# Attention projection's weights split in six parts inside head pairs 2 to 4, and its first row block's product laid in four pieces into the attention's drain

## What is computed

```python
h = _ln(x, ln1_g, ln1_b)
q, k, v = (einsum('btd,hds->bhts', h, W) for W in (Wq, Wk, Wv))
att = softmax(where(causal, q @ k.T * d ** -0.5, -inf))
out = (att @ v).transpose(0, 2, 1, 3).reshape(b, t, d)
x = x + out @ Wp + bp                  # the attention projection
h2 = _ln(x, ln2_g, ln2_b)
w, sel = top_k(h2 @ Wg, 1)             # the gate: one expert for each token
y = relu(h2 @ W1[sel] + b1[sel]) @ W2[sel] + b2[sel]
```

## Time and profile before

| | |
|---|---|
| median of 3 runs | 899.28 us (898.9 to 900.07) |
| the profiled execution | 897.33 us |
| its span | 895.8 us |
| PE busy | 850.7 us, 95% |
| DVE busy | 711.0 us, 79% |
| ACT busy | 553.0 us, 62% |
| attention's last head pair, from its first scores | 345.78 us on |
| first matmul of the projection | 383.26 us |
| first matmul of the experts | 444.39 us |

### The profile page before, as it was taken

One profiled execution on the slowest core, in us unless ns is written; L12 is line 12 of the kernel. 1 busy time (PEld: TensorE's weight loads), 2 busy tenths in 40 slices (PEclk: granted clock), 3 DMA queues, 4 the chain that ended last, 5 costly groups with the idle time before them and its releaser, 6 DMA issues.

```text
span 895.8 us, 14645 instructions
## 1 busy us (share of the span) xinstructions
PE 850.7 (95%) x5342; PEld 820.7 (92%) x5342; DVE 711.0 (79%) x1093; ACT 553.0 (62%) x783; POOL 80.1 (9%) x85
## 2 busy tenths in 40 slices
PE   6999999999999998799999999999999999999997
PEld 6989999999888887699899999999999999999996
DVE  6999676863687767734779798898989989898995
ACT  3612341353667667611678787787878888787870
POOL 2000000330400000022330000000000000000040
PEclk9999999999999999899999999999999999999998
DMA  7130008164810102730499999999999999999984
GB/s 197 40 106 1 19 10 168 53 175 89 334 54 2 54 1 70 227 89 2 130 357 350 372 334 372 355 359 378 342 379 367 358 373 354 376 354 371 367 279 135
DMA packets 116232, 196.00 MB, mean 219 GB/s; under 512 B 34052, under 2 KB 83420, under 8 KB 116182
## 3 DMA queue, kind: packets, MB, share of 16 engines
q1 hardware_dynamic: 107988, 169.08, 55.9%
q0 software_dynamic: 6368, 24.19, 8.0%
q10 hardware_dynamic: 1826, 2.06, 0.8%
HBM read 177.40 MB, written 17.90 MB: 218 GB/s over the span
## 4 chain that ended last, share of the span: by engine, by line
PE 52%; DVE 22%; DMA 14%; issue 6%; ACT 6%; SPq 0%; DVEq 0%; ACTq 0%
PE ps L1480 14%; DVE wlo L988 13%; DMA raw<-in_L_ffn_W 12%; PE ps L1874 7%; PE ps L1657 7%; PE ps L1855 6%; PE ps L1733 3%; ACT whi L658 2%; PE ps L1561 2%; PE ps L1587 2%; PE ps L1696 2%; PE ps L1711 2%; PE ps L1509 2%; DMA xs<-in_x 1%; DVE hTT L986 1%
## 5 line engine op out<-in xcount | busy, mean ns | idle before, releaser
L988 DVE TENSOR_TENSOR wlo<-raw,whi 128x2304 fp32r<-128x2304 f32 (+2 forms) x148 | 352.6, 2390 | 24.5 <-ACT whi L658 24.1
L658 ACT ACTIVATE whi<-raw 128x2304 fp32r<-128x2304 f32 (+2 forms) x150 | 300.4, 2004 | 80.0 <-DMA raw<-in_L_ffn_W 34.6
L1874 PE MATMUL ps<-whi,hTT 128*128 128x384 f32 x768 | 201.6, 339 | 1.0 <-ACT oh7T L658 1.0
L1874 PEld LDWEIGHTS ps<-whi,hTT 128*128 128x128 f32 x768 | 139.2, 188 | 1.2 <-ACT oh7T L658 1.2
L1855 PE MATMUL ps<-whi,hgh 128*128 128x384 f32 x384 | 133.1, 347 | 1.3 <-DVE hgl L988 1.3
L1855 PE MATMUL ps<-whi,hgl 128*128 128x384 f32 x384 | 129.1, 336 | 0.0
L1874 PE MATMUL ps<-wlo,hTT 128*128 128x384 f32 x384 | 129.0, 336 | 0.0
L1855 PE MATMUL ps<-wlo,hgh 128*128 128x384 f32 x384 | 128.4, 334 | 0.0
L1855 PEld LDWEIGHTS ps<-whi,hgh 128*128 128x128 f32 x384 | 72.2, 188 | 1.5 <-DVE hgl L988 1.5
L1874 PEld LDWEIGHTS ps<-wlo,hTT 128*128 128x128 f32 x384 | 72.3, 188 | 0.0
L1855 PEld LDWEIGHTS ps<-wlo,hgh 128*128 128x128 f32 x384 | 72.3, 188 | 0.0
(11 more groups left out here) (287 smaller groups left out, 1642.8 us busy)
## 6 DMA issues: line engine op xcount, KB each, us to landing
raw<-in_L_ffn_W SPq DMA_DIRECT2D x128, 1152.0 KB, 7.0
hs_d<-bc POOLq DMA_DIRECT2D x13, 384.0 KB, 6.4
raw<-in_L_gnn_W SPq DMA_DIRECT2D x4, 1152.0 KB, 6.3
hs<-hs_d POOLq DMA_DIRECT2D x8, 384.0 KB, 5.6
ys_d<-ysb POOLq DMA_DIRECT2D x7, 384.0 KB, 6.0
raw<-in_L_ffn_Wv SPq DMA_DIRECT2D x6, 384.0 KB, 5.5
raw<-in_L_ffn_Wq SPq DMA_DIRECT2D x12, 192.0 KB, 3.4
raw<-in_L_ffn_Wk SPq DMA_DIRECT2D x12, 192.0 KB, 3.3
```

What stands on the lines that cost most here:

```text
L658: act.activation(out_, in_, func).then_inc(s, 1)
L988: dve.tensor_tensor(out_, in_, hi_, ALU.subtract).then_inc(s, 1)
L1874: ins = mm(ps[0:CAP, 4 + half, 0:HB], l, rr, start=k == 0 and j == 0 and jj == 0, stop=k == FCH - 1 and j == JW - 1 and jj == 2)
```

## The change

The Wp split becomes six parts of 768 columns, in steps 14, 16, 17, 20, 22 and 24 (WP_AT). Each takes the place in `whi`/`wlo` and the third of `raw` that one unit had (WP_PLACE), and waits until that unit's products are done (WP_USED). Three of the last units change their place (UNIT_PLACE), and unit 11 is split in step 18 where it was in step 14. SP's second Wp load goes out after unit 11 and so four steps later; the experts' first chunk goes out after the third Wp part, in step 17, the second after the sixth, in step 24.

The product of row block 0 leaves the loop after the drain. Its 36 matmuls are four pieces of 9 (`first_block`): at the head of step 29, at the head of step 30, behind step 30's turns, and at the head of step 31. The six keep-busy matmuls go. The banks of the five blocks become 0, 2, 4, 6, 4 (WP_BANK), and the waits follow the banks: the first piece waits for all maxima (its banks held scores), for all six Wp parts and for the heads of row block 0; block 4 waits for block 2's residual, gate products for block 1's.

```diff
-UNIT_PLACES = 6
-UNIT_SLOT = (0, 0, 1, 1, 0, 1)
-UNIT_COL = (0, D, 0, D, 2 * D, 2 * D)
+UNIT_PLACE = (0, 1, 2, 3, 4, 5, 0, 1, 2, 3, 5, 2)
+RAW_PLACES = 6
+PLACE_SLOT = (0, 0, 1, 1, 0, 1)
+PLACE_COL = (0, D, 0, D, 2 * D, 2 * D)
-UNIT_AT = {1: 6, 4: 7, 6: 8, 9: 9, 11: 10, 14: 11}
+UNIT_AT = {1: 6, 4: 7, 6: 8, 9: 9, 11: 10, 18: 11}
-WP_PARTS = 4
+WP_AT = {14: 0, 16: 1, 17: 2, 20: 3, 22: 4, 24: 5}
+WP_PLACE = (0, 1, 4, 3, 5, 2)
+WP_USED = (16, 16, 16, 20, 22, 24)
+WP_BANK = (0, 2, 4, 6, 4)
+WP_QUARTER = 9
-WP_AT = STEPS - 6
-DRAIN_BUSY = 3
...
             def wp_hi(k):
-                n, part = divmod(k, WP_PARTS // 2)
-                if not k:
-                    a.wait_ge(s_pj, C + 4 * PAIRS)
+                p = WP_PLACE[k]
+                n = PLACE_SLOT[p]
+                a.wait_ge(s_pj, C + WP_USED[k])
                 a.wait_ge(s_raw[n], raw_value(2 * WP + n))
-                cols = slice(part * CH // 2, (part + 1) * CH // 2)
-                hi(front_w[n][0][:, cols], raw[n][:, cols], s_fhi)
+                hi(place(p, front_w)[0], raw[n][:, PLACE_COL[p]:PLACE_COL[p] + D], s_fhi)
...
+            def first_block(k):
+                if not k:
+                    pe.wait_ge(s_mx, 2 * STEPS)
+                    pe.wait_ge(*split(FRONT + 4))
+                    pe.wait_ge(s_pvl, 2 * (STEPS - C + 1))
+                order = {0: 0, 1: 1, 3: 2, 2: 3}[k]
+                for a_ in range(order * WP_QUARTER, (order + 1) * WP_QUARTER):
+                    half, a_m = divmod(a_, QK)
+                    m, i = divmod(a_m, 3)
+                    l, rr = pairs([t[:, m, 0:P] for t in q],
+                                  [t[:, half * HB:(half + 1) * HB] for t in wpart(2 * WP, m)])[i]
+                    ins = mm(ps[0:P, WP_BANK[0] + half, 0:HB], l, rr, start=a_m == 0, stop=a_m == QK - 1)
+                if order == 3:
+                    ins.then_inc(s_wp, 1)
...
-                if i >= STEPS:
-                    keep_busy(DRAIN_BUSY, v[0][:, 0, 0:128], v[0][:, 0, 0:512], 0)
+                if i >= STEPS - 1:
+                    first_block(i - STEPS + 1)
                 if 1 <= i <= STEPS:
                     turn(2 * i - 2)
                     turn(2 * i - 1)
+                if i == STEPS:
+                    first_block(3)
...
             for c in range(C):
+                if c == 4:
+                    pe.wait_ge(s_x2, 3)
+                if c:
+                    rows_product(q, 2 * WP, c, WP_BANK[c], {DC - 1: (s_pvl, 2 * STEPS)} if c == 1 else None
+                                 ).then_inc(s_wp, 1)
                 if c >= 2:
-                    pe.wait_ge(s_x2, c - 1)
-                rows_product(q, 2 * WP, c, 4 + 2 * (c % 2), None if c else {DC - 1: (s_pvl, 2 * STEPS)}).then_inc(s_wp, 1)
-                if c >= 2:
+                    if c == 2:
+                        pe.wait_ge(s_x2, 2)
                     gate_products(c - 2)
```

More of the change, by code:

```diff
@@ L311, in unit, with place @@
         def unit(j, tensors):
-            p = j % UNIT_PLACES
-            return [t[:, UNIT_COL[p]:UNIT_COL[p] + D] for t in tensors[UNIT_SLOT[p]]]
+            return place(UNIT_PLACE[j], tensors)
+        def place(p, tensors):
+            return [t[:, PLACE_COL[p]:PLACE_COL[p] + D] for t in tensors[PLACE_SLOT[p]]]
         def raw_unit(j):
-            return raw[j % UNIT_PLACES // 3][:, j % 3 * D:(j % 3 + 1) * D]
+            return raw[j % RAW_PLACES // 3][:, j % 3 * D:(j % 3 + 1) * D]
         def unit_count(j):
@@ L347, in build @@
         s_fhi, s_flo = sem("front_hi"), sem("front_lo")
-        s_unit = [sem(f"qk_weight_in{p}") for p in range(UNIT_PLACES)]
+        s_unit = [sem(f"qk_weight_in{p}") for p in range(RAW_PLACES)]
         s_uhi, s_ulo = sem("qk_weight_hi"), sem("qk_weight_lo")
@@ L481, in _ @@
                 m, r = divmod(j, 2)
[L482 to L483 removed]
+                if j >= RAW_PLACES:
+                    sp.wait_ge(s_ulo, unit_count(j - RAW_PLACES))
                 else:
@@ L498, in weights @@
                     elif n < F_RAWS:
-                        sp.wait_ge(*split(2 * WP + WP_PARTS // 2 * (n + 1)))
+                        sp.wait_ge(*split(2 * WP + 3 * (n + 1)))
                     else:
@@ L780, in unit_hi @@
             def unit_hi(j):
-                a.wait_ge(s_unit[j % UNIT_PLACES], 32 * (j // UNIT_PLACES + 1))
-                if j >= UNIT_PLACES:
-                    a.wait_ge(s_pj, C + 2 * (j - UNIT_PLACES) + 2)
+                a.wait_ge(s_unit[j % RAW_PLACES], 32 * (j // RAW_PLACES + 1))
+                held = [n for n in range(j) if UNIT_PLACE[n] == UNIT_PLACE[j]]
+                if held:
+                    a.wait_ge(s_pj, C + 2 * held[-1] + 2)
                 else:
-                    a.wait_ge(*USED[(GNN2, WV)[UNIT_SLOT[j]]])
+                    a.wait_ge(*USED[(GNN2, WV)[PLACE_SLOT[j]]])
                 hi(unit(j, front_w)[0], raw_unit(j), s_uhi)
@@ L874, in _ @@
                     unit_hi(UNIT_AT[i])
-                if 0 <= i - WP_AT < WP_PARTS:
-                    wp_hi(i - WP_AT)
+                if i in WP_AT:
+                    wp_hi(WP_AT[i])
                 if i % C in QK_LATE and window_pair(i) < PAIRS:
@@ L1218, in wp_lo @@
             def wp_lo(k):
-                n, part = divmod(k, WP_PARTS // 2)
+                p = WP_PLACE[k]
+                n = PLACE_SLOT[p]
                 d.wait_ge(s_fhi, 2 * WP + k + 1)
-                w_hi, w_lo = front_w[n]
-                cols = slice(part * CH // 2, (part + 1) * CH // 2)
-                lo(w_lo[:, cols], raw[n][:, cols], w_hi[:, cols], s_flo)
+                w_hi, w_lo = place(p, front_w)
+                lo(w_lo, raw[n][:, PLACE_COL[p]:PLACE_COL[p] + D], w_hi, s_flo)
             def maximum(u):
@@ L1282, in _ @@
                     unit_lo(UNIT_AT[i])
-                if 0 <= i - WP_AT < WP_PARTS:
-                    wp_lo(i - WP_AT)
+                if i in WP_AT:
+                    wp_lo(WP_AT[i])
                 if i % C in QK_LATE and window_pair(i) < PAIRS:
@@ L1297, in _ @@
                 d.wait_ge(s_wp, c + 1)
-                dve.tensor_tensor(x2[:, c, :].rearrange("p (a b) -> p a b", a=2), wide(4 + 2 * (c % 2), P),
+                dve.tensor_tensor(x2[:, c, :].rearrange("p (a b) -> p a b", a=2), wide(WP_BANK[c], P),
                                   xfb[:, c, :].rearrange("p (a b) -> p a b", a=2), ALU.add).then_inc(s_x2, 1)
@@ L1751, in _ @@
                     values(i - 2)
-            pe.wait_ge(s_pvl, 2 * (STEPS - C))
             pe.wait_ge(s_trl, 2 * STEPS)
-            pe.wait_ge(*split(2 * WP + WP_PARTS))
             def turn_n2(c):
```

4 lines of the change are left out of this document (1 added, 3 removed).

## The result

| | before | after |
|---|---|---|
| median | 899.31 us (898.9 to 900.07, 4 executions) | 888.01 us (886.88 to 893.28, 4 executions) |
| the profiled execution | 897.33 us, span 895.8 | 887.97 us, span 886.4 |
| last pair's first scores | 345.78 us | 347.75 us |
| first turns of step 29 | 370.91 us | 368.06 us |
| product of row block 1 | 389.58 us | 378.99 us |

The ratio is 0.988, with a 95% interval of 0.9853 to 0.9908: 11.3 us faster, where 9.8 were forecast, and inside the forecast's range. Two later comparisons of the same kernel, of six executions each, have 0.9894 and 0.9891, that is 9.4 and 8.7 us. The mean over all 16 executions of the change is 889.7 and over 39 of the kernel before, from the later comparisons, 899.5: **9.8 us**.

A forecast was written before the change was run, and what follows sets the result against it. PE alone was taken to bound the projection, and PE held by DVE and ACT the last pair and drain. -6.3 - 4.3 + 0.1 + 0.4 + 0.3 = -9.8 took 899.28 to 889.5 us, range 887.3 to 893.2.

The forecast's parts named there:

- Row block 0 leaves the loop: Projection loop after the drain: row block 0's 36 matmuls no longer stand there, -6.3 us.
- The last pair without the splits: Steps 24 to 28: waits behind the Wp splits on DVE and ACT go, -4.3 us, bounds 1.7 and 8.3.
- more is won: Rival, last pair: a second low-clock stretch vanishes or the last pair's gain is nearer 6; 887.5 us, chance 0.06.
- The drain: Step 29's turns to last `values`: +6.3 for matmuls, -1.0 wait, -2.1 keep-busy, -1.2 idle, -1.9 clock, together +0.1 us.
- about 12.3: Sign of being right: the drain from step 29's turns to the last `values` still takes about 12.3 us.
- Splits in pairs 2 to 4: Moved splits cost nothing except in step 18, ahead of k's low part: +0.4 us, bounds 0 and 3.6.
- Changes of kind: PE's queue around the pieces: some eight changes of kind at under 0.1 each, +0.3 us (0 to 0.6).
- Queues: Later second Wp load, earlier expert chunks, POOL's `base` load and new bank waits: nothing.
- the clock stays low in the drain: Rival, drain: clock stays low under the pieces, making the drain's term +3.3 and the time 892.7 us; chance 0.17.
- Another wait takes the place of the splits: Rival, last pair: PE waits as long for the ring's next member, gain only 1.7, time 892.1 us; chance 0.10.
- Slower: Rival, pairs 2 to 4: all seven splits are on the path and cost 12.6 us, time 901.7 us; chance 0.02.
- A part of the gain given back by the experts' full transfers: Sign of being wrong: a drain shorter by the whole gain and an expert stretch longer by it.

The follow-up runs named there:

- experiment 9: The kernel before, nothing edited, profiled a second time: 898.28 us, one execution.
- split alone: The change with PE's side put back, so only the six-part Wp split stays: 894.57 us, ratio 0.9944 to the kernel before.
- experiment 8: The kernel before with 25 keep-busy matmuls added in its last pair's waits: 898.25 us beside 898.96, ratio 0.9988.
- experiment 4: The change with unit 11 split in step 19 instead of 18 and the fourth Wp part in step 21 instead of 20: 890.19 us, ratio 0.9906.
- experiment 1: The change, nothing edited, run a second and a third time: 890.41 us, ratio 0.9894, and 890.28 us, ratio 0.9891.
- experiment 5: The change with only the 12 high by high matmuls of row block 0's 36: 889.02 us, ratio 0.9875.
- experiment 7: The change with nine keep-busy matmuls in step 25: 886.22 us, ratio 0.9845; the same with unit 11 in step 19: 888.84 us, ratio 0.988.
- experiment 6: The change with unit 11 in step 19 and half of row block 0's product in steps 25, 28 and 29: 886.32 us, again 885.24 us.

## Why the prediction was right

The forecast was -9.8 and the mean of all executions is -9.8, the first comparison's -11.3. That the two agree to the tenth is luck; that they agree within 2 us is not. The change's three profiles have a mean stretch of 87.1 and the two of before 98.0, so -10.9; pair 3 adds 0.4, and the last 40 matmuls happened to take 1.8 us more in the change's profiles (experiment 9), which no term had. By terms:

1. *Row block 0 leaves the loop, -6.3.* Right: 389.58 - 383.26 = 6.3 in the profile before, and block 1's 36 matmuls (6.28 in the chain) now follow the last `values` without a wait.

2. *The last pair without the splits, -4.3.* Right in the mean, and the reason given was right: the waits for the heads' low parts are gone. Step 29's turns come 4.8 us sooner, although the first piece delays them by 0.6, as forecast: DVE's instruction behind the last maximum begins at 366.25, and by the 370.91 - 369.72 = 1.2 of before the turns could have begun at 367.4. So it is 5.4 without the piece. The same reckoning gives 3.9 for the second run of the change and 3.3 for the third, which have the low clock in step 25; the mean is 4.2. The steps can be read one by one, in PE's starts behind the pair's first scores:

| | before | split alone | change, second run | change, first run |
|---|---|---|---|---|
| turns of the last keys, step 25 | 7.90 | 7.49 | 7.50 | 7.49 |
| next scores | 11.09 | 10.05 | 10.76 | 9.29 |
| `values` that waited for step 25's heads | 12.77 | 11.73 | 11.92 | 10.44 |
| next `values`, step 26's heads | 17.99 | 14.99 | 15.15 | 13.66 |
| next `values`, step 27's heads | 22.59 | 18.33 | 18.63 | 17.15 |

In the second run, whose clock is low in the same place as before, the steps give 0.4, 0.5, 2.0 and 1.1 us, together 4.0, where the prediction had 0.4, 0.5, 2.1 and 1.3. The first run has the same four and 1.5 more from the clock, between the first row and the second. The term was worked out as if the clock there were the same before and after, and that is so in two of the change's three profiles only; the rival "more is won" had this case, at 2 us and a chance of 0.06, which was too small.

3. *The drain, +0.1.* Its additions and removals came as laid out. From the turns to row block 1 the profile before has 18.7 us and the change 10.9, so -7.7. Piece by piece: block 0 -6.3, 27 matmuls of the pieces +4.8, keep-busy -2.1, idle -1.2, turns and `values` of step 29 at full clock -1.9: each as predicted. (By its own terms the prediction should have looked for 11.8 us from the turns to the last `values`, since 0.6 of the first piece lies ahead of the turns; its sign of "about 12.3" left that out. Measured is 10.9.) **What was missed** is step 30's turns, which the low stretch to 377.3 also covered: from their start to the next instruction's they took 1.6 before and take 0.8 now. The sum left them out, so the clock was worth 2.7 and not 1.9 beside the keep-busy matmuls. In the kernel before itself it is worth less: experiment 8 has 2.3 with the keep-busy matmuls, since waits take a part back there; in the change the pieces fill them.

4. *Splits in pairs 2 to 4, +0.4.* Right, in place and size: 26.00 us against 25.62, and gone with experiment 4. The other splits cost nothing: the changed pairs' other periods are 25.6 to 25.7.

5. *Changes of kind, +0.3.* Smaller: from start to start the second and the fourth piece take 1.58, 0.175 a matmul, the one behind the turns 374.04 - 372.38 = 1.66 and the first, behind a wait, 1.68. That is 0.2 in all, within the 0 to 0.6.

6. *Queues, 0.* Right: PE, ACT and DVE waited for no Wp load, and from the first gate products to the experts it is 41.4 us as before.

The rule of the Trainium skill's page "TensorE: Matmul & The Clock Gate", section "Back-to-back issue gap", would have a piece of nine at 1.46 us. The page gives it for an isolated matmul and says that it comes out too high for wide matmuls in a stream. The trace after does not agree either: 1.58, so here it comes out too low.

Of the rivals, *the clock stays low in the drain* did not come in any of the change's three profiles. The Trainium skill's page "TensorE: Matmul & The Clock Gate", section "What's actually happening", has the point of change move between runs. Experiments 1 and 9 agree (354 to 358 us at 0.50 in one run of the change and at 1.00 in another), but in step 25 rather than under the pieces. *Another wait takes the place of the splits* did not come in the last pair (its list before has eight waits and not seven, of which five are left); in the drain the waits return only when work is taken out (experiment 5). *Slower* never was near: one of seven splits reached the path.

The first comparison's 11.3 against 9.4 and 8.7 of the later ones goes mostly with the clock: with one of four executions in the slower group the median lies in the faster one (888.0), with three of six, twice, between the two (890.4 and 890.3). The means differ by 0.9 only, 889.0 against 890.0 and 889.9. A part of the gain given back by the experts' full transfers (share 1.02 in both) isn't seen. The experts took 1.3 us longer in the change's first profile than in the first before, but up to the last 40 matmuls they were 0.4 shorter (435.9 against 436.3), and those took 2.1 longer at their lower clock. Over all profiles of the two kernels what lies ahead of the last 40 is 0.7 longer in the change, which is within its scatter.

What stays open is why the clock falls in one execution and not in another.

## What to carry to other kernels

Put real work where waits are: a drain in which three engines pass one item round has room for matmuls that need only finished data, up to the ring's own length (at most 10.9 us here), and what goes beyond costs its time. A split of weights is free in steps where the tensor engine has other work and on the path where it has not, unless it stands right ahead of an instruction that this engine waits for; look for that instruction in each step, not for the engine's mean load. When a low clock is priced, go through every instruction in the low stretch, to its end, and then look for the next wait, which can take the gain back. Before a difference between two profiles is explained, compare the clock at the end of the program too.

## What the runs showed of the hardware that was not expected

The granted clock of one and the same program differs between executions in place: step 25 ran at 2.4 GHz in one profile of the change and partly at 1.2 GHz in two, at 1.5 to 2.1 us a time. In those two PE was busy for 1.4 and 1.8 of the 3.3 us from 350.0 to 353.3 us, just ahead of the fall, and in the one without a fall for 2.1 of the same 3.3. The last 40 matmuls took 9.3 to 13.0 us with it. A good half of the scatter between executions (correlation -0.74) goes with the clock.

What a low stretch costs depends on what follows it. The one in step 25 cost 1.5 us where PE's work came next (experiment 1) and 0.3 where PE next waited for a split on DVE (experiment 8); the one over the drain cost 2.3. Holding the clock with useless matmuls cost nothing in waits that stay waits (experiment 7) and won nothing that the times can tell in the kernel before (experiment 8). Work that has to be done anyway held it as well and shortened the stretch by 1.4 us more (experiment 6).
